# A decoder block in one launch: region fills, bias table, Newton steps and rank products in other places

## The reference, cut to what matters

```python
x = x + tanh(g_xattn[0]) * cross_attention(layernorm(x), ctx)   # 32 query heads, 8 key heads of 128
x = x + tanh(g_ffn[0])   * permuted_head_ffn(layernorm(x))      # 16 heads of 32, gelu
x = x + tanh(g_xattn[1]) * group_attention(layernorm(x), ctx)   # 8 groups, group norm
x = x + tanh(g_ffn[1])   * experts(layernorm(x))                # 8 experts of 512 x 512, top 1

def experts(x):                       # the part that the change is mostly about
    logits = xf @ gate_w.T + gate_b
    selected = argmax(softmax(logits))
    out = sum over j of where(selected == j, xf @ expert_w[j].T + expert_b[j], 0)
```

## Time and profile before

| what | value |
|---|---|
| median of 3 runs | 843.44 us |
| the profiled execution's own time | 843.73 us |
| its span, first to last instruction | 841.9 us |
| mean granted TensorE clock | 0.951 |
| PE busy | 761.2 us (90%) |
| DVE, ACT, POOL busy | 470.9, 481.3, 306.4 us |
| chain that ended last | PE 79%, DVE 5%, ACT 4%, DMA 4%, issue 4%, POOL 2% |

### The profile page before, as it was taken

One profiled execution on the slowest core, in us unless ns is written; L12 is line 12 of the kernel. 1 busy time (PEld: TensorE's weight loads), 2 busy tenths in 40 slices (PEclk: granted clock), 3 DMA queues, 4 the chain that ended last, 5 costly groups with the idle time before them and its releaser, 6 DMA issues.

```text
span 841.9 us, 13494 instructions
## 1 busy us (share of the span) xinstructions
PE 761.2 (90%) x3893; PEld 605.5 (72%) x3893; DVE 470.9 (56%) x890; ACT 481.3 (57%) x1816; POOL 306.4 (36%) x623
## 2 busy tenths in 40 slices
PE   6999967999999997999999899999999988543997
PEld 4888855888888886888887788888887624222775
DVE  4875304565565563655654555556566646746642
ACT  5453226766667664677675576676655456561631
POOL 1330005444353352353353244435323257522222
PEclk9999988999999998999999899999999979865999
DMA  8635551014015006005105101401220156713131
GB/s 300 202 106 162 185 195 63 14 56 184 14 45 193 17 14 213 25 12 204 34 13 184 42 13 58 179 13 58 79 98 2 50 189 240 322 52 127 46 106 63
DMA packets 42125, 87.76 MB, mean 104 GB/s; under 512 B 5561, under 2 KB 26041, under 8 KB 38226
## 3 DMA queue, kind: packets, MB, share of 16 engines
q1 hardware_dynamic: 38884, 78.71, 27.6%
q0 software_dynamic: 3184, 8.41, 2.8%
HBM read 70.28 MB, written 35.57 MB: 126 GB/s over the span
## 4 chain that ended last, share of the span: by engine, by line
PE 79%; DVE 5%; ACT 4%; DMA 4%; issue 4%; POOL 2%; SPq 1%; POOLq 0%; ACTq 0%; DVEq 0%
PE banks L857 7%; PE banks L858 7%; PE banks L859 7%; PE banks L829 6%; PE banks L828 6%; PE banks L827 6%; PE banks L817 6%; PE banks L836 4%; PE banks L400 3%; PE banks L398 3%; PE banks L844 3%; PE banks L399 3%; PE banks L1729 2%; PE banks L1730 2%; PE banks L1731 2%
## 5 line engine op out<-in xcount | busy, mean ns | idle before, releaser
L577 ACT ACTIVATE p_sb<-p_sb,nmax 128x128 f32<-128x128 f32 x256 | 99.7, 391 | 132.7 <-DVE nmax L751 132.7
L670 POOL TENSOR_TENSOR v_lo<-v_raw,v_hi 128x128 fp32r<-128x128 f32 x64 | 29.7, 464 | 272.3 <-ACT v_hi L615 272.3
L817 PEld LDWEIGHTS banks<-kT,qT_sb 128*128 128x128 f32 x512 | 67.7, 193 | 7.3 <-ACT qT_sb L585 2.0
L774 DVE TENSOR_TENSOR pT_lo<-banks,pT_hi 128x512 fp32r<-128x512 f32 x64 | 44.3, 692 | 51.0 <-ACT pT_hi L590 51.0
L817 PE MATMUL banks<-kT,qT_sb 128*128 128x128 f32 x512 | 68.5, 277 | 1.4 <-ACT qT_sb L585 1.4
L675 POOL TENSOR_TENSOR p_sb<-p_sb,rsum 128x512 f32<-128x512 f32 x64 | 66.6, 1041 | 5.6 <-DVE rsum L770 5.6
L742 DVE TENSOR_TENSOR oT_lo<-banks,oT_hi 128x512 fp32r<-128x512 f32 x64 | 44.1, 688 | 43.5 <-ACT oT_hi L572 43.4
L622 ACT ACTIVATE q_junk<-banks 128x128 f32<-128x128 f32 x256 | 66.2, 274 | 0.0
L572 ACT ACTIVATE oT_hi<-banks 128x512 fp32r<-128x512 f32 x64 | 38.1, 595 | 47.3 <-PE banks L870 35.8
L780 DVE SCALAR_TENSOR_TENSOR x_sb<-banks,tgates,x_sb 128x512 f32<-128x512 f32 x64 | 48.1, 751 | 23.8 <-PE banks L859 23.8
L398 PE MATMUL banks<-w_hi,ctx_hi 128*128 128x512 f32 x128 | 54.3, 424 | 7.5 <-DVE ctx_lo L329 7.4
(11 more groups left out here) (267 smaller groups left out, 2126.0 us busy)
## 6 DMA issues: line engine op xcount, KB each, us to landing
sorted_x<-in_empty SPq DMA_DIRECT2D x8, 2064.0 KB, 9.3
w_raw<-in_wq_l SPq DMA_DIRECT2D x8, 1024.0 KB, 11.5
w_raw<-in_wo_l SPq DMA_DIRECT2D x8, 1024.0 KB, 6.9
exp_w<-in_exp_w_l SPq DMA_DIRECT2D x8, 1024.0 KB, 8.9
kT_scr<-kT_st SPq DMA_DIRECT2D x16, 256.0 KB, 2.3
v_scr<-v_st SPq DMA_DIRECT2D x16, 256.0 KB, 2.4
xs<-sorted_x SPq DMA_DIRECT2D x15, 258.0 KB, 2.9
v_raw<-v_scr SPq DMA_DIRECT2D x14, 256.0 KB, 2.5
```

The costliest lines, as they stand in the source:

```text
L577: last = act.activation(p_sb[:, b % 2, h * P:(h + 1) * P], p_sb[:, b % 2, h * P:(h + 1) * P], ACT.Exp, bias=nmax[:, b % 2, h:h + 1], accum ...
L817: last = pe.matmul(s_ps[:, h * P:(h + 1) * P], qT_sb[:, b % 2, h * P:(h + 1) * P], kT[:, b * P:(b + 1) * P], start=True, stop=True)
```

## The change

- `fill(g)` is issued after `kT_half(0)` instead of after `kT_half(1)`; `fill(0)` goes from the front to behind the loads for the gate. The load of `exp_b` follows the wo load of group 1, and the split of the bias goes into steps 6 (ACT) and 7 (DVE) of group 0.
- The bias product gets 128 rows: `ones_r` is 128 x 128 ones, `exp_b2` has 128 partitions, ACT writes zeros over all of it after its four splits of weights (a new column `zero`), and SP loads the two real rows over them once that is done.
- POOL runs rstd(1) ahead of scatter(0). PE runs ranks(0) ahead of logits(1).
- ACT's list in the tile loop has `normalise` ahead of `split_x`.

```diff
@@ attention, SP
                 sp.dma_start(wo_raw[:, :, :], d.wo[g, :, :, :]).then_inc(wo_ld, 16)
+                if isinstance(g, int):
+                    sp.dma_start(s.exp_b[:, :], d.exp_b).then_inc(s.exp_b_ld, 16)
                 v_half(0)
                 kT_half(0)
+                fill(g)
                 v_half(1)
                 kT_half(1)
-                fill(g)
...
-            fill(0)
-            sp.dma_start(s.exp_b[:, :], d.exp_b).then_inc(s.exp_b_ld, 16)
             loads(1)
...
                 sp.dma_start(dst, src).then_inc(s.gate_ld, 16)
+            fill(0)
             sp.wait_ge(s.exp_b_split, 2)
@@ attention, ACT (DVE likewise, with b == B - 1, for the low part)
-            act.wait_ge(s.exp_b_ld, 16)
-            act.activation(s.exp_b_hi[:, :], s.exp_b[:, :], ACT.Copy).then_inc(s.exp_b_split, 1)
+            def split_bias(u, b, g, odd):
+                if isinstance(g, int) and g == 0 and b == B - 2:
+                    act.wait_ge(s.exp_b_ld, 16)
+                    act.activation(s.exp_b_hi[:, :], s.exp_b[:, :], ACT.Copy).then_inc(s.exp_b_split, 1)
@@ attention, DVE
+            dve.memset(s.zero[:, :], 0.0).then_inc(s.ones_set, 1)
+            dve.wait_ge(s.ones_set, 3)
+            dve.tensor_copy(s.ones_r[:, :], s.ones[:, :]).then_inc(s.ones_set, 1)
@@ experts, SP
-            sp.wait_ge(logit_done, 2)
-            sp.dma_start(s.exp_b2[:, :, :].bitcast(F32), d.exp_b2).then_inc(exp_b_ld, 16)
+            sp.wait_ge(bias_zeroed, 1)
+            sp.dma_start(s.exp_b2[0:2, :, :].bitcast(F32), d.exp_b2).then_inc(exp_b_ld, 16)
@@ experts, ACT
+            act.wait_ge(gateT_done, 2)
+            act.activation(s.exp_b2[:, :, :], s.zero[:, 0:1].unsqueeze(2).to_broadcast([P, E, D]), ACT.Copy)\
+                .then_inc(bias_zeroed, 1)
...
-            run([(split_x, 1), (normalise, 2), (split_next_w, 3)])
+            run([(normalise, 2), (split_x, 1), (split_next_w, 3)])
@@ experts, POOL
             rstd(0)
+            rstd(1)
             pool.wait_ge(s.filled, 16 * E)
             pool.wait_ge(s.token_set, 2)
             scatter(0)
-            rstd(1)
             scatter(1)
@@ experts, PE
             gates(1)
-            logits(1)
...
             ranks(0)
+            logits(1)
             ranks(1)
@@ tiles
-        s.ones_r = m.sb("ones_r", [2, P], F32R)
+        s.ones_r = m.sb("ones_r", [P, P], F32R)
...
-            s.exp_b2, s.xn = beside("exp_b2", [2, E, D], 0, F32R), beside("xn", [P, 2, D], 24)
+            s.exp_b2, s.xn = beside("exp_b2", [P, E, D], 0, F32R), beside("xn", [P, 2, D], 24)
```

More of the change, by code:

```diff
@@ L662, in _ @@
             run(act, [(oT_split, -2), (exps, 0), (copy_z01, 0), (qT_copy, 1), (pT_split, -1), (copy_z2, -1), (copy_z3, -1),
-                      (v_split, 2), (q_stats, 2), (seed_ln2, -3), (copy_xT, -6)]
+                      (v_split, 2), (q_stats, 2), (seed_ln2, -3), (copy_xT, -6), (split_bias, 0)]
                 + [(wq_split(kt), 7 - kt) for kt in range(KT)] + [(wo_split(h), 4 - h) for h in range(HG)])
@@ L729, in _ @@
             dve.memset(s.gate_c[:, :, :], 0.0).then_inc(s.ones_set, 1)
-            dve.wait_ge(s.ones_set, 2)
-            dve.tensor_copy(s.ones_r[:, :], s.ones[0:2, :]).then_inc(s.ones_set, 1)
+            dve.memset(s.zero[:, :], 0.0).then_inc(s.ones_set, 1)
+            dve.wait_ge(s.ones_set, 3)
+            dve.tensor_copy(s.ones_r[:, :], s.ones[:, :]).then_inc(s.ones_set, 1)
             for k in range(EXTRA):
@@ L735, in _ @@
             dve.tensor_copy(s.mT[:, :], oT_ps[:, 0:P]).then_inc(mT_copied, 1)
-            dve.wait_ge(s.exp_b_split, 1)
-            dve.tensor_tensor(s.exp_b_lo[:, :], s.exp_b[:, :], s.exp_b_hi[:, :].bitcast(F32), ALU.subtract)\
-                .then_inc(s.exp_b_split, 1)
             def oT_split(u, b, g, odd):
@@ L788, in x_stats, with split_bias @@
                         layernorm_var(dve, s, x_step, 2 * (b + 1), slice(b + 1 - HB, b + 1)).then_inc(xval_done, 1)
+            def split_bias(u, b, g, odd):
+                if isinstance(g, int) and g == 0 and b == B - 1:
+                    dve.wait_ge(s.exp_b_split, 1)
+                    dve.tensor_tensor(s.exp_b_lo[:, :], s.exp_b[:, :], s.exp_b_hi[:, :].bitcast(F32), ALU.subtract)\
+                        .then_inc(s.exp_b_split, 1)
             def copy_xT(u, b, g, odd):
@@ L806, in _ @@
             run(dve, [(oT_split, -2), (mask_max, 0), (q_scale, 1), (p_recip, 0), (pT_split, -1), (q_half, 2),
-                      (copy_xT, -6), (normalise_ln2, -5), (accumulate, -2), (x_stats, -2)])
+                      (copy_xT, -6), (normalise_ln2, -5), (accumulate, -2), (x_stats, -2), (split_bias, 0)])
         @block.tensor
@@ L1185, in _ @@
             dve.wait_ge(s.gate_ld, 16 * GATE_LOADS)
-            dve.wait_ge(s.ones_set, 3 + EXTRA)
+            dve.wait_ge(s.ones_set, 4 + EXTRA)
             dve.scalar_tensor_tensor(out=s.gate_c[:, :, 0:E], in0=sm_ps[:, 320:320 + E].unsqueeze(1).to_broadcast([P, KT, E]),
@@ L1302, in _ @@
             pe.wait_ge(s.gate_ld, 16 * GATE_LOADS)
-            pe.wait_ge(s.ones_set, 3)
+            pe.wait_ge(s.ones_set, 4)
             for kt in range(KT):
@@ L1361, in experts @@
         w_hi_done, w_lo_done = m.sem("ew_hi_done"), m.sem("ew_lo_done")
-        exp_b_ld = m.sem("exp_b2_ld")
+        exp_b_ld, bias_zeroed = m.sem("exp_b2_ld"), m.sem("bias_zeroed")
         y_done, res_done = m.sem("ey_done"), m.sem("eres_done")
@@ L1807, in flamingo @@
         s.rows_before, s.upto = m.sb("rows_before", [P, P]), m.sb("upto", [P, E, E])
+        s.zero = m.sb("zero", [P, 1])
         s.ones, s.steps, s.fold = m.sb("ones", [P, P]), m.sb("steps", [P, EXTRA]), m.sb("fold", [P, E])
-        s.ones_r = m.sb("ones_r", [2, P], F32R)
+        s.ones_r = m.sb("ones_r", [P, P], F32R)
         s.exp_b = s.at("exp_b", [E, D], 112)
```

## The result

The changed kernel takes 805.74 us, the median of 4 runs (804.71 to 806.6), beside 843.54 for the kernel before on the same chip (4 runs, 842.59 to 844.87): a ratio of 0.955, 95% interval 0.9532 to 0.9569. The profiled execution took 806.6 us, with a span of 804.8 and a mean granted clock of 0.970 (0.951 before).

A forecast was written before the change was run, and what follows sets the result against it. PE, 90% busy, was taken as the bound: time is won only where it idles, runs at its lower clock or overspends on products. Gains 8.9 + 10.2 + 8.7 + 1.0 + 5.5 - 0.5 = 33.8 from 843.7 gave 809.9 us, range 802.5 to 821.

The forecast's parts named there:

- Start, -8.9: Start of the attention: with the bias split moved out, ACT's squares start 6.9 us earlier and the clock stays up; 8.9 us gained.
- Fills, -10.2: Hardware loop's two jumps: code fetch meets nearly empty DMA engines once the fill moves mid-group; 5.1 us each, 10.2 in all.
- rival A: Loop jumps: the 5.69 us wait is the fetch itself, so the fills gain nothing; 820.1 us, chance 0.15.
- rival C: Loop jumps: with the fill moved, the jump costs nothing; 804.6 us, chance 0.15.
- Rival D: Mid-group: the moved 2 MB fill delays code fetches in seven groups, making the kernel slower; 863 us, chance 0.03.
- Newton and ranks, -8.7: Routing: the reordered Newton step and ranks let the last four scatters and the tile loads start 8.7 us earlier.
- even at twice that price ACT is free: Routing: ACT's zeros over the bias table, 4.2 us, end at 759.4, before the first tile at 763.8.
- Normalise first, -1.0: First tile: normalise no longer queues behind the first split, so the experts' first product starts earlier; 1.0 us gained.
- Bias product, -5.5: Expert tiles: 128 rows remove idle weight loads around the bias product, 0.35 us for each of fourteen tiles plus 0.6; 5.5 us.
- rival B: Expert tiles: the bias product's rows do not cause the gaps, which stay; 815.4 us, chance 0.10.
- the 1.6 us of backlog fit: Expert tiles: DVE needs 3.9 us a tile, PE 3.5; the splits' one-tile lead absorbs the 1.6 us backlog.
- Clock at the first tile, +0.5: First expert tiles: PE's clock may return later in the new order, costing 0.5 us (-0.2 to +1.5).

## Why the prediction came out as it did

The direction and the range held: 809.9 was forecast, 805.74 came. In units of the profiled execution, 33.8 us of gain were forecast and 37.1 found.

- **Start, -8.9: mis-sized.** 7.9 in the trace, some of it the address, and 7.5 when done alone. ACT's squares and PE's idle time came out as forecast (118.69 with the split alone; 0.96). What failed is "the clock should stay up": eight matmuls of the next product ran at the lower level in spite of the short gap, and the term is near its low end.
- **Fills, -10.2: mechanism right, size 12.3.** Each long group lost 6.0 to 6.3, and 1.3 more in the changed kernel is the address. I took 3 us for a fetch from free engines; ACT waits 2.0 to 2.3. The clock was spared, as forecast: a long group with the fills alone is 1.6 to 1.7 us over the others, little more than PE's stall of 1.4. So rival A (the 5.69 are the fetch itself) falls, and so does C (a jump costs nothing). About 2 us are what is left of the cost of a taken jump. This agrees with the forced fetch of which the Trainium skill speaks (Runtime: NRT & Kernel Launch, section Instruction fetch mechanics). The section gives no latency, and here load on the DMA engines made it nearly three times as long. How much of the load was the fill and how much the wq load behind it was not tried.
- **Rival D** (fills that delay fetches in mid-group) falls by the groups at 64.11 us with the fills alone.
- **Newton and ranks, -8.7: right**, 8.7 when done alone, 5.8 of it from the Newton step (10.1 to 10.4 and 7.1 to 7.4 against the profiles where the clock falls later). In the changed kernel it is 7.8. What I had not costed is the place of the table's load: "even at twice that price ACT is free" is right for ACT (the zeros took 3.60 us, not 4.2, and ended at 733.97), but SP, which waits for the zeros, then issues the table just ahead of the first tile. From the last scatter to the first normalise it takes 6.56 us, where it was 6.08, and 5.94 with the load moved behind: about half of the shortfall of 0.9. The other half lies ahead of the last scatter, which comes 24.4 us behind the first transpose and 24.0 with the two moves alone: the fifth scatter waits 0.75 us for its rows, and the last two take 1.50 instead of 0.97 beside DVE's splits.
- **Normalise first, -1.0: right** at its stage; the whole time gained 2.6, and what the rest is the profiles don't show. Its side effect was not foreseen: ACT, now ahead, waits for tile loads.
- **Bias product, -5.5: right at the turn, not at the end.** 0.39 a turn, and 14 x 0.39 = 5.5; rival B falls. The Trainium skill's rule of equal times for a single product with 32 and with 128 rows (TensorE: Matmul & The Clock Gate, section Why this matters for your kernels), carried over to 2 rows, would have made it 0; the run with 2 rows measures 5.9 in the tiles, so the measurement decides. The Trainium skill (TensorEngine Tiling (Array Packing), section Key Properties) says that a change of tiling mode drains TensorE. The idle weight loads around the 2-row product look like that; whether a product of 2 rows is such a change no run here shows. In the profile of the changed kernel only 3.6 came, clock included, and 5.9 in a second one: the step "the 1.6 us of backlog fit" looked at DVE and forgot what a faster tile and an ACT that runs ahead ask of the next resource, six buffers that are free only when their stores have landed. With seven the stage gains 65.0 - 58.2 = 6.8.
- **Clock at the first tile, +0.5: wrong sign.** PE came back to 0.39 us a matmul 3.6 us after its first product, 5.6 us before. That is 2.0 us less at the lower level, where a matmul has a pitch of 0.43 instead of 0.23: a gain of 0.9.
- **The address: not seen at all**, 4.2 to 4.7 us, the largest miss. The diff adds a tile of 4 bytes, and I read it for its value and not for what it pushes along. By stages: 0.66 in a group, and if all eight are like the four that were measured, 5.3 in all, an estimate.

The sum by stages: 7.5 + 12.3 + 7.8 + 1.0 + 3.6 + 5.3 = 37.5, less 1.4 for the later beginning, is 36.1; 1.0 us of the 37.1 stays without a cause. The time fell on rival C's 804.6, though C is false: a number close to the result says nothing of its reasons. By ratios, on the other chips: the bias split 0.86%, the fills 1.28, Newton and ranks 1.20, normalise 0.30, the address 0.55 and the 128 rows 0.48 (0.9573 - 0.9525) make 4.67%, and the whole change has 4.75%.

## What to carry to other kernels

When a change shortens the step of a pipeline, or lets one engine run ahead in it, go around its ring: a buffer is busy from its load until its store has landed, and a ring that was just long enough becomes the bound. Large transfers should not be under way where a hardware loop jumps, since its code must come through the same engines. And an edit that declares a new tile may move every tile behind it: time that shift alone, before the rest of the change is given the credit.

## What the runs showed of the hardware that was not expected

- **Addresses of TensorE's operands.** In the output projection, whose weights alone moved, products of 512 columns have a pitch of 0.228 us with weights that begin at a multiple of 64 bytes and 0.233 with weights 32 bytes past one: 2%. Moving the tiles is worth 0.5% of the kernel, shown in both directions. It is no general figure: the experts' products went from 0.234 to 0.232.
- **A scatter that POOL issues can take 2.5 times as long beside DVE.** POOL's store of a tile and DVE beside it:

```profile
755.04 1.26 POOL L1492 DMA_INDIRECT out<-xs  x1 [2.45 <-DVE xs L1651]
758.70 2.46 POOL L1492 DMA_INDIRECT out<-xs  x1 [2.40 <-DVE xs L1651]
762.36 2.46 POOL L1492 DMA_INDIRECT out<-xs  x1 [1.20 <-DVE xs L1651]
```

```profile
754.15 2.49 DVE L1599 TENSOR_TENSOR ew_lo<-exp_w,ew_hi 128x512 fp32r<-128x512 f32 x4
...
761.48 2.49 DVE L1599 TENSOR_TENSOR ew_lo<-exp_w,ew_hi 128x512 fp32r<-128x512 f32 x4
763.89 0.68 DVE L1645 TENSOR_TENSOR xsT_lo<-banks,xsT_hi 128x512 fp32r<-128x512 f32 x1
```

All three issues begin 0.9 us after the first of four splits of weights on DVE. The first takes 1.26 us, as such issues do at most in the kernel before; the others take 2.46 and end 0.9 us after the last split, as if they had waited for it. With DVE idle it is 0.98. What makes the difference between 1.26 and 2.46 stays open. The Trainium skill (SBUF — State Buffer, section SBUF: two separate sides) says that POOL, which writes the descriptors, is locked out of a shared port while DVE holds it. The long issues agree with that, the short one beside the same splits does not by itself; no run here takes DVE's work away. The 1.2 us lengthen the time for which a tile's buffer is taken.
- **The price of a jump** is 2.0 to 2.3 us of waiting on ACT with free DMA engines and 5.1 to 6.6 beside 3 MB of transfers.
